# Score products of the second attention layer issued for two jobs at a time in every second slot of TensorE

## The chip, the cores and the metric

The kernel runs on one core of one Trainium2 chip. The metric is device time in microseconds (us), and a lower one is better. The profile is one execution taken by the hardware profiler; its engines are TensorE (PE, its weight loads PEld), VectorE (DVE), ScalarE (ACT), GpSimd (POOL) and the DMA queues that SyncE (SP) issues.

## The reference, cut to what matters

Two layers are computed on a tensor of 4 x 512 tokens with 256 features: an attention that learns as it reads, a feed-forward net, a causal attention with 16 heads, and a routed expert net. The change lies in the third of these, whose core is

```python
scores = jnp.einsum('bqhd,bkhd->bhqk', q, k) * scale        # 128 "nope" + 64 "rope" features
scores = jnp.where(causal[None, None], scores, jnp.finfo(scores.dtype).min)
probs = jax.nn.softmax(scores, axis=-1)
out = jnp.einsum('bhqk,bkhd->bqhd', probs, v).reshape(b, s, NH * D_V)
return out @ Wo
```

The 128 nope features of a key come from a latent of 64 numbers, so the kernel multiplies the key weights into the query first. A score is then a product over 64 latent features plus a product over 64 rope features.

## The kernel before

**Tiling.** `stage_rest` works on 16 batches n (`batches`), each one sample b and one tile of 128 query rows q, in the order q = 1, 3, 0, 2 of each sample. Because of the causal mask a batch needs 128 x (q + 1) keys, so the widths are 256, 512, 128 and 384 for n mod 4 = 0, 1, 2, 3. A batch has eight jobs of two heads, p = 0 to 7; job t = 8n + p, 128 in all (`SLOTS`). Each engine walks through the slots t = 0 to 127 in an order written out by hand.

**A job on the engines.** `score(t)` issues four products on TensorE: latent and rope part for heads e = 0 and e = 1, whose operands lie in rows 0 to 63 and 64 to 127 (lines 2098 and 2101). They go to one of two pairs of PSUM banks (`t % AHEAD`). On VectorE, `largest(t)` (L2454) moves the two score tiles to SBUF and finds their row maxima (`maxed`), `turn(t - 2)` (L2468) transposes the finished probabilities of job t - 2, and `invert(t)` (L2473) takes reciprocals of the sums. On ScalarE, `exponential(t)` (L2354) makes the exponentials. On GpSimd, `normalize(t)` (L2707) scales them. `score(t)` reuses the banks of job t - 2 and waits for `maxed` of job t - 2, head by head.

**Fills.** The rest of TensorE's work is put between the scores by `Plan`, by slot p of the batch: at p = 0, 1 the rope queries of batch n + 1 (L2056, `project_q`); at 2, 3 the weighing of the values of batch n - 1 (`weigh`, L2118, products of 32 rows; one part at p = 2 where n mod 4 = 3); at 4, 5 (3, 4 where n mod 4 = 3) the latent queries of batch n + 1 (L2056); at 6, 7 the output product of batch n - 1 (`project_out`, L2132), at 6, 7 of n mod 4 = 0 also the next sample's values (L2064), at 6 of n mod 4 = 2 its keys (L2073, 64 rows), and at 7 of n = 0, 2, 6, 10, 14 transposes of a norm (L1591). Batch 0 has no weighing and no output; batch 15 makes no queries, and has its output product at 3, 4. Fills use four other banks in turn.

**What the other engines do with a fill.** In its slot, ScalarE first does `exponential(t)`, then takes what was filled in slot t - 1 (`take_rope` L2342, `take_latent` L2346, the value rows L1979, the keys L2334, a norm L1604), and takes the weighed sum (`take_out`, L2363, semaphore `oT_taken`) in the slot after the last part of `weigh`. It is strictly in order, so `exponential(t + 1)` stands behind these takes. On VectorE, the gating of an output (`gate_out`, L2494) stands at the end of slot p = 0, before `largest` of p = 1; the rotation of the keys (L2483, L2484) in slot p = 1 of n mod 4 = 3; the rotation of rope queries (L2479) in p = 4, 5; sums and normalization of a norm (L1566, L1584) in p = 1 and p = 4 of n = 0, 2, 6, 10, 14. The first latent fill and `project_out` need `oT_taken`.

Of the kernel before, what the change touches and what calls it, by code (L numbers as in the profile page):

```python
# [1826 lines left out]
def stage_rest(k):  # L1827
# [8 lines left out]
    AHEAD = 2  # L1836
# [4 lines left out]
    SLOTS = NP * NB  # L1841
# [99 lines left out]
    def wait_taken(eng, *what):  # L1941
        eng.wait_ge(taken[banks.bank(*what)], banks.count(*what))
# [12 lines left out]
    def width(n):  # L1955
        return P * (batches[n][1] + 1)
# [28 lines left out]
    with nc.Block() as block:  # L1985
        @block.tensor
        def _(pe):
# [63 lines left out]
            def project_q(what, w, n, half):  # L2051
                b, cols = tokens(n)
                out = claim(what, n, half)
                for i in range(HP):
                    for kt in range(KT):
                        mm = nc.tensor.matmul(out[:, P * i:P * i + P], w[:, kt, HP * half + i, :], k.hT[:, kt, b, cols],  # L2056
                                              start=(kt == 0), stop=(kt == KT - 1))
                mm.then_inc(made_of(what, n, half), 1)

            def project_value(b, half):  # L2060
                out = claim("value", b, half)
                pe.wait_ge(norms.taken, norms.done(LN1A + b, 1))
                for kt in range(KT):
                    mm = nc.tensor.matmul(out[:], w_val[kt][:, P * half:P * half + P], k.hT[:, kt, b, :],  # L2064
                                          start=(kt == 0), stop=(kt == KT - 1))
                mm.then_inc(made_of("value", b, half), 1)
# [9 lines left out]
            def turn_norm(g):  # L2076
                for kt in range(KT):
                    out = claim("norm", g, kt)
                    norms.turn(pe, g, kt, out)

            def score(t):
                n, p = divmod(t, NP)
                b = batches[n][0]
                if t == 0:
                    pe.wait_ge(first_rows, 2)
                if t == 1:
                    pe.wait_ge(gated_made, 2 * len(ITEMS))
                if p % HP == 0:
                    wait_taken(pe, "latent", n, p // HP)
                    pe.wait_ge(s["q_roped"], 2 * n + p // HP + 1)  # L2090
                    if n % QT == 0:
                        pe.wait_ge(s["ckv_taken"], 2 * (b + 1))
                        pe.wait_ge(keys_spread[p // HP], MOVE * (b + 1))
                halves = [slice(LORA * e, LORA * e + LORA) for e in range(2)]
                for e, rows in enumerate(halves):
                    if t >= AHEAD:
                        pe.wait_ge(s["maxed"], 2 * (t - AHEAD) + e + 1)
                    nc.tensor.matmul(score_bank[t % AHEAD][e][:, 0:width(n)], q_latent[rows, n % 2, p, :],  # L2098
                                     ckvT[rows, b % 2, 0:width(n)], start=True, stop=False)
                for e, rows in enumerate(halves):  # L2100
                    nc.tensor.matmul(score_bank[t % AHEAD][e][:, 0:width(n)], q_rope[rows, n % 2, p, :],  # L2101
                                     keys[b % 2][rows, p // 2, 0:width(n)], start=False, stop=True).then_inc(s["scored"], 1)

            def weigh(n, part, parts):
                b, blocks = batches[n][0], blocks_of(n)
                lo, hi = blocks * part // parts, blocks * (part + 1) // parts
                if part == 0:
                    pe.wait_ge(s["turned"], NP * (n + 1))
                    if b > 0:
                        wait_taken(pe, "value", b, 1)  # L2110
                    for last in banks.before_sum(n):
                        clear(last)
                src = turned_of[batches[n][1]]
                for j in range(lo, hi):
                    for e in range(2):
                        for i in range(ROWS):
                            rows = slice(BLK * i, BLK * i + BLK)
                            mm = nc.tensor.matmul(av[LORA * e:LORA * e + LORA, i, :], val[rows, b % 2, j, :], src[rows, j, e, :, :],  # L2118
                                                  start=(j == 0), stop=(j == blocks - 1))
                if part == parts - 1:  # L2120
                    mm.then_inc(s["weighed"], 1)

            def project_out(n, part):
                out = filled("out", n)
                if part == 0:
                    if n < NB - 1:
                        clear(banks.previous("out", n))
                    pe.wait_ge(s["oT_taken"], n + 1)
                elif n == NB - 1:
                    pe.wait_ge(s["oT_taken"], NB + 1)  # L2130
                for p in range(HP * part, HP * part + HP):
                    mm = nc.tensor.matmul(out[:, 0:D], oT[:, p, :], w_vo[:, p, :], start=(p == 0), stop=(p == NP - 1))  # L2132
                if part == 1:
                    mm.then_inc(made_of("out", n), 1)
# [112 lines left out]
            for n, (b, q) in enumerate(batches):  # L2247
                m, more = n % QT, n + 1 < NB
                for p in range(NP):
                    t = NP * n + p  # L2250
                    if t + AHEAD < SLOTS:
                        score(t + AHEAD)
                    part = p - plan.weigh[m]
                    if n > 0 and 0 <= part < plan.parts[m]:
                        weigh(n - 1, part, plan.parts[m])
                    for half in range(2):
                        if n > 0 and p == plan.out_at(n)[half]:
                            project_out(n - 1, half)
                    for half in range(2):
                        if more and p == plan.rope[m][half]:  # L2260
                            project_q("rope", w_rope, n + 1, half)
                        if more and p == plan.latent[m][half]:
                            project_q("latent", w_abs, n + 1, half)
                    for half in range(2):
                        if b + 1 < B and m in plan.value and p == plan.value[m][half]:
                            project_value(b + 1, half)
                    if b + 1 < B and m in plan.key and p == plan.key[m]:
                        project_keys(b + 1)
                    if n in plan.norms and p == plan.norm:
                        turn_norm(plan.norms[n])  # L2270
# [662 lines left out]
```

## Time and profile before

| | before |
|---|---|
| median of 3 runs | 1076.84 us (1074.63 to 1078.26) |
| profiled execution, its own time | 1076.94 us |
| its span | 1075.1 us |
| PE busy in the span | 1016.1 us (95%) |
| DVE busy | 703.8 us (65%) |
| ACT busy | 546.1 us (51%) |
| POOL busy | 433.7 us (40%) |
| the change's stretch, first score to last | 575.5 to 1018.4 us |

A row of a timeline reads: start, duration, engine, line, operation, output <- inputs, shapes, count, and in brackets how long the engine had been idle before it and what released it. Successive matmuls overlap in their listed durations, so the time that one costs TensorE is the distance to the start of the next.

### The profile page before, as it was taken

How to read it: one execution, taken by the hardware profiler on the slowest of the kernel's cores; microseconds unless marked ns; L12 is line 12 of the kernel's file. 1: busy time of each engine (PE TensorE's matmuls, PEld its weight loads, DVE VectorE, ACT ScalarE, POOL GpSimd, SP SyncE). 2: the span in 40 equal slices, each digit the busy share in tenths (PEclk: the TensorE clock that was granted, in tenths of full speed). 3: DMA queues.
4: the chain of work that ended last, by engine and by line, in shares of the span. 5: the costliest groups of instructions: out<-in, count | busy, mean ns of one | idle time of the engine just before them, and what ended most of it. 6: DMA issues, size and time to landing. Idle time of an engine off the chain costs nothing.

```text
span 1075.1 us, 25979 instructions
## 1 busy us (share of the span) xinstructions
PE 1016.1 (95%) x10226; PEld 739.7 (69%) x10226; DVE 703.8 (65%) x2121; ACT 546.1 (51%) x1418; POOL 433.7 (40%) x391
## 2 busy tenths in 40 slices
PE   6788999999999999999999999999999999999978
PEld 4567888888878546655667576766767686758646
DVE  4888898898899713122225675747584767667774
ACT  2667777777778531212132543545454545444441
POOL 1222033134145411010106474747475756778610
PEclk9999999999999999999999899999999999999999
DMA  9150000000000009100013011200120003000202
GB/s 322 44 185 2 1 0 0 0 0 0 1 2 2 1 1 294 46 1 1 1 30 70 15 27 31 64 7 21 36 65 22 21 22 79 22 21 22 80 2 80
DMA packets 27887, 44.03 MB, mean 41 GB/s; under 512 B 6928, under 2 KB 16912, under 8 KB 26896
## 3 DMA queue, kind: packets, MB, share of 16 engines
q1 hardware_dynamic: 27792, 42.71, 13.5%
q8 instruction: 66, 1.08, 0.4%
q14 instruction: 29, 0.24, 0.1%
HBM read 21.98 MB, written 2.10 MB: 22 GB/s over the span
## 4 chain that ended last, share of the span: by engine, by line
PE 53%; DVE 5%; ACT 2%; issue 1%; POOL 0%; DVEq 0%
PE quad L2056 10%; PE quad L1705 8%; PE quad L2098 7%; PE quad L2118 7%; PE quad L2101 6%; PE quad L2000 5%; PE quad L2132 5%; PE quad L2196 1%; PE quad L2064 1%; ACT act_probs L2354 1%; PE quad L1591 1%; DVE act_probs L2454 1%; ACT act_probs L2363 1%; PE quad L2019 1%; DVE x_pairs L2484 1%
## 5 line engine op out<-in xcount | busy, mean ns | idle before, releaser
L2707 POOL TENSOR_TENSOR act_probs<-act_probs,rden 128x512 f32<-128x512 f32 (+3 forms) x128 | 171.0, 1339 | 155.7 <-DVE rden L2473 155.6
L2354 ACT ACTIVATE act_probs<-act_probs,neg_max 128x256 f32<-128x256 f32 (+3 forms) x256 | 140.8, 552 | 82.9 <-DVE neg_max L2454 82.6
L2056 PEld LDWEIGHTS quad<-hT,ug_queries 128*128 128x128 f32 x1024 | 120.5, 194 | 30.6 <-issue 18.6
L2056 PE MATMUL quad<-hT,ug_queries 128*128 128x128 f32 x1024 | 132.2, 283 | 3.0 <-ACT act_probs L2363 2.2
L2454 DVE CUSTOM_DVE_ANT_0 act_probs<-quad,mask 128x256 f32<-128x256 f32 (+3 forms) x256 | 115.1, 486 | 6.8 <-PE quad L2101 6.1
L1705 PE MATMUL quad<-hT,ug_raw_switch 128*128 128x512 f32 x256 | 115.8, 602 | 0.0
L2098 PE MATMUL quad<-ckvT,ug_raw_switch 64*128 64x512 f32 (+3 forms) x512 | 105.8, 480 | 6.9 <-DVE neg_max L2454 6.9
L2473 DVE RECIPROCAL rden<-den 128x2 f32<-128x2 f32 x128 | 20.6, 161 | 120.2 <-ACT act_probs L2354 120.1
L1720 DVE SCALAR_TENSOR_TENSOR act_probs<-quad,ws_up,silu_keys 128x512 f32<-128x512 f32 x32 | 24.0, 750 | 102.4 <-ACT silu_keys L1715 102.4
L1705 PEld LDWEIGHTS quad<-hT,ug_raw_switch 128*128 128x128 f32 x256 | 48.0, 192 | 55.7 <-issue 55.5
L1715 ACT ACTIVATE silu_keys<-quad,ws_gate 128x512 f32<-128x512 f32 x32 | 22.0, 687 | 120.5 <-PE quad L1705 120.5
L2468 DVE STREAM_TRANSPOSE wq_wo<-act_probs 128x1024 f32<-128x1024 f32 (+1 forms) x64 | 70.8, 1106 | 3.1 <-POOL act_probs L2707 3.1
L2098 PEld LDWEIGHTS quad<-ckvT,ug_raw_switch 64*128 64x128 f32 x512 | 41.7, 186 | 39.8 <-issue 20.6
L2132 PE MATMUL quad<-down_keys,act_probs 128*128 128x256 f32 x256 | 63.5, 392 | 0.8 <-ACT act_probs L2363 0.8
L1426 POOL TENSOR_TENSOR hidden<-gate_silu,hb 128x256 f32<-128x256 f32 x16 | 12.0, 753 | 124.5 <-ACT hb L969 124.5
L2132 PEld LDWEIGHTS quad<-down_keys,act_probs 128*128 128x128 f32 x256 | 46.1, 189 | 19.2 <-issue 11.4
L2000 PE MATMUL quad<-down_raw_out,act_probs 128*128 128x256 f32 x256 | 56.1, 379 | 2.0 <-PEq L1510 2.0
L2000 PEld LDWEIGHTS quad<-down_raw_out,act_probs 128*128 128x128 f32 x256 | 48.4, 190 | 10.1 <-issue 3.7
L2118 PE MATMUL quad<-wq_wo,latent_rows 32*64 32x256 f32 x1792 | 53.0, 378 | 2.4 <-DVE ug_raw_switch L2500 1.6
L1206 DVE SCALAR_TENSOR_TENSOR q_bf<-quad,silu_keys 128x512 bf16<-128x512 f32 x72 | 46.2, 683 | 5.3 <-PE quad L645 5.1
L2354 ACT ACTIVATION_READ_ACCUMULATOR act_probs<-act_probs,neg_max 128x1 f32 x256 | 48.3, 189 | 0.0
L2118 PEld LDWEIGHTS quad<-wq_wo,latent_rows 32*64 32x64 f32 x1792 | 41.0, 131 | 10.3 <-issue 3.6
(332 smaller groups left out, 2317.6 us busy)
## 6 DMA issues: line engine op xcount, KB each, us to landing
rope_swapped<-gate SPq DMA_DIRECT2D x120, 64.0 KB, 2.0
ug_raw_switch<-in_wmod SPq DMA_DIRECT2D x4, 512.0 KB, 6.3
x_pairs<-in_x SPq DMA_DIRECT2D x4, 512.0 KB, 7.0
x_rows<-x_pairs SPq DMA_DIRECT2D x8, 256.0 KB, 5.0
wq_wo<-in_wq_nopeT SPq DMA_DIRECT2D x1, 2048.0 KB, 8.6
wq_wo<-in_wo SPq DMA_DIRECT2D x1, 2048.0 KB, 12.8
down_raw_out<-x_pairs SPq DMA_DIRECT2D x16, 128.0 KB, 2.3
ug_queries<-in_switch_w SPq DMA_DIRECT2D x1, 2048.0 KB, 7.6
```

Of the source, the lines that this page charges most:

```text
L1206: nc.vector.scalar_tensor_tensor(q_bf[:, q, :], bank[q][:], ca_b2, a_bf[:, q, :], ALU.mult, ALU.add).then_inc(taken[q], 1)
L1705: mm = k.nc.tensor.matmul(k.bank[2 * (m % 2) + w][:], self.w_ug[:, w, kt, P * m:P * m + P], k.hT[:, kt, 2 * i:2 * i + 2, 4 * C * u:4 * C * ...
L2000: mm = nc.tensor.matmul(bank[4 + q // 2][:, D * (q % 2):D * (q % 2) + D], act_t[:, m, P * q:P * q + P], w_down[:, ffn.place(m), :], start= ...
L2056: mm = nc.tensor.matmul(out[:, P * i:P * i + P], w[:, kt, HP * half + i, :], k.hT[:, kt, b, cols], start=(kt == 0), stop=(kt == KT - 1))
L2098: nc.tensor.matmul(score_bank[t % AHEAD][e][:, 0:width(n)], q_latent[rows, n % 2, p, :], ckvT[rows, b % 2, 0:width(n)], start=True, stop=F ...
L2101: nc.tensor.matmul(score_bank[t % AHEAD][e][:, 0:width(n)], q_rope[rows, n % 2, p, :], keys[b % 2][rows, p // 2, 0:width(n)], start=False, ...
L2118: mm = nc.tensor.matmul(av[LORA * e:LORA * e + LORA, i, :], val[rows, b % 2, j, :], src[rows, j, e, :, :], start=(j == 0), stop=(j == bloc ...
L2132: mm = nc.tensor.matmul(out[:, 0:D], oT[:, p, :], w_vo[:, p, :], start=(p == 0), stop=(p == NP - 1))
L2354: nc.scalar.activation(tile, tile, ACT.Exp, bias=neg_max[:, r, e:e + 1], scale=-1.0, accum_out=den[:, r, e:e + 1])\
L2454: nc.vector.tensor_tensor_reduce(probs[:, t % RING, e, 0:cols], score_bank[t % AHEAD][e][:, 0:cols], mask[:, L - cols:L], -QK_SCALE, 3e38, ...
L2468: nc.vector.transpose(turned_of[batches[n][1]][:, :, :, p, :].rearrange("p j e c -> p e j c"), probs[:, t % RING, :, 0:width(n)].rearrange ...
L2707: nc.gpsimd.tensor_tensor(tile, tile, rden[:, t % RING, :].unsqueeze(2).to_broadcast([P, 2, cols]), ALU.mult)\
```

## The change

At every even slot t, TensorE now issues `score(t + 2)` and `score(t + 3)` one behind the other, and at odd slots none; the fills of slots t and t + 1 then follow each other. The waits inside `score` are as before, so the second of the pair waits for `maxed` of job t + 1, and the number of products is the same. The other engines' programs are the same.

```diff
                 for p in range(NP):
                     t = NP * n + p
-                    if t + AHEAD < SLOTS:
+                    if t % 2 == 0 and t + AHEAD < SLOTS:
                         score(t + AHEAD)
+                        score(t + AHEAD + 1)
                     part = p - plan.weigh[m]
```

TensorE from p = 4 of batch 1 (width 512) to p = 7, before: ckvT products (L2098) and key products (L2101) are the scores, `hT,ug_queries` the latent queries, `down_keys,act_probs` the output product.

```order
L2098 MATMUL quad<-ckvT,ug_raw_switch 128x512 x2
L2101 MATMUL quad<-silu_keys,ug_raw_switch 128x512 x2
L2056 MATMUL quad<-hT,ug_queries 128x128 x8
L2098 MATMUL quad<-ckvT,ug_raw_switch 128x512 x2
L2101 MATMUL quad<-silu_keys,ug_raw_switch 128x512 x2
L2056 MATMUL quad<-hT,ug_queries 128x128 x8
L2098 MATMUL quad<-ckvT,ug_raw_switch 128x128 x2
L2101 MATMUL quad<-silu_keys,ug_raw_switch 128x128 x2
L2132 MATMUL quad<-down_keys,act_probs 128x256 x4
L2098 MATMUL quad<-ckvT,ug_raw_switch 128x128 x2
L2101 MATMUL quad<-silu_keys,ug_raw_switch 128x128 x2
L2132 MATMUL quad<-down_keys,act_probs 128x256 x4
```

The same slots of the changed kernel:

```order
L2098 MATMUL quad<-ckvT,ug_raw_switch 128x512 x2
L2101 MATMUL quad<-silu_keys,ug_raw_switch 128x512 x2
L2098 MATMUL quad<-ckvT,ug_raw_switch 128x512 x2
L2101 MATMUL quad<-silu_keys,ug_raw_switch 128x512 x2
L2056 MATMUL quad<-hT,ug_queries 128x128 x16
L2098 MATMUL quad<-ckvT,ug_raw_switch 128x128 x2
L2101 MATMUL quad<-silu_keys,ug_raw_switch 128x128 x2
L2098 MATMUL quad<-ckvT,ug_raw_switch 128x128 x2
L2101 MATMUL quad<-silu_keys,ug_raw_switch 128x128 x2
L2132 MATMUL quad<-down_keys,act_probs 128x256 x8
```

The first score of batch 2's second job moved ahead of both output products, and the two latent fills stand together behind both scores.

TensorE from p = 2 of batch 3 (width 384) to the scores of batch 4 (width 256), before:

```order
L2098 MATMUL quad<-ckvT,ug_raw_switch 128x384 x2
L2101 MATMUL quad<-silu_keys,ug_raw_switch 128x384 x2
L2118 MATMUL quad<-x_pairs,latent_rows 64x256 x32
L2098 MATMUL quad<-ckvT,ug_raw_switch 128x384 x2
L2101 MATMUL quad<-silu_keys,ug_raw_switch 128x384 x2
L2056 MATMUL quad<-hT,ug_queries 128x128 x8
L2098 MATMUL quad<-ckvT,ug_raw_switch 128x384 x2
L2101 MATMUL quad<-silu_keys,ug_raw_switch 128x384 x2
L2056 MATMUL quad<-hT,ug_queries 128x128 x8
L2098 MATMUL quad<-ckvT,ug_raw_switch 128x384 x2
L2101 MATMUL quad<-silu_keys,ug_raw_switch 128x384 x2
L2098 MATMUL quad<-ckvT,ug_raw_switch 128x256 x2
```

and in the changed kernel:

```order
L2118 MATMUL quad<-x_pairs,latent_rows 64x256 x32
L2056 MATMUL quad<-hT,ug_queries 128x128 x8
L2098 MATMUL quad<-ckvT,ug_raw_switch 128x384 x2
L2101 MATMUL quad<-silu_keys,ug_raw_switch 128x384 x2
L2098 MATMUL quad<-ckvT,ug_raw_switch 128x384 x2
L2101 MATMUL quad<-silu_keys,ug_raw_switch 128x384 x2
L2056 MATMUL quad<-hT,ug_queries 128x128 x8
L2098 MATMUL quad<-ckvT,ug_raw_switch 128x256 x2
L2101 MATMUL quad<-down_raw_out,ug_raw_switch 128x256 x2
```

The first latent fill now stands right behind the weighing, and the second right before the scores of the next batch; before, a score stood between them in both places.

## Rows read from the trace of the kernel before

**Rows 1.** Busy time in a window: window, length, PE, PEld, DVE, ACT, POOL, PEclk, DMA.

```profile
680.00:780.00 100.00, 99.07 (x1099) 69.79 (x1095) 61.67 (x197) 47.66 (x140) 59.94 (x49) 1.00 0.13 30
```

**Rows 2.** Timeline of PE, two rope slots of batch 9 (width 512).

```profile
839.73 1.13 PE L2098 MATMUL quad<-ckvT,ug_raw_switch 64*128 64x512 f32 x4
...
841.65 2.05 PE L2056 MATMUL quad<-hT,ug_queries 128*128 128x128 f32 x16
843.63 1.13 PE L2098 MATMUL quad<-ckvT,ug_raw_switch 64*128 64x512 f32 x4
```

**Rows 3.** Timeline of PE: a score behind a score, and one between fills, width 256.

```profile
576.44 0.60 PE L2098 MATMUL quad<-ckvT,ug_raw_switch 64*128 64x256 f32 x4
...
577.30 0.38 PE L2098 MATMUL quad<-ckvT,ug_raw_switch 64*128 64x256 f32 x1
...
804.66 0.70 PE L2098 MATMUL quad<-ckvT,ug_raw_switch 64*128 64x256 f32 x4
...
805.73 2.05 PE L2056 MATMUL quad<-hT,ug_queries 128*128 128x128 f32 x16
```

**Rows 4.** Timeline of PE: a value fill behind a score, and one behind a fill.

```profile
600.22 1.12 PE L2064 MATMUL quad<-hT,wk_nopeT 128*128 128x512 f32 x2
...
602.14 0.70 PE L2098 MATMUL quad<-ckvT,ug_raw_switch 64*128 64x512 f32 x2
...
828.46 1.02 PE L2064 MATMUL quad<-hT,wk_nopeT 128*128 128x512 f32 x2
...
830.27 0.70 PE L2098 MATMUL quad<-ckvT,ug_raw_switch 64*128 64x512 f32 x2
```

**Rows 5.** Timeline, batch 9 to 10: latent take, exponential, reciprocal, maxima, next score.

```profile
855.29 0.60 ACT L2346 ACTIVATE ug_raw_switch<-quad 128x512 f32<-128x512 f32 x1 [1.40 <-PE quad L2056]
855.79 0.71 ACT L2354 ACTIVATE act_probs<-act_probs,neg_max 128x512 f32<-128x512 f32 x1
...
857.33 0.17 DVE L2473 RECIPROCAL rden<-den 128x2 f32<-128x2 f32 x1 [0.27 <-ACT act_probs L2354]
857.45 0.69 DVE L2454 CUSTOM_DVE_ANT_0 act_probs<-quad,mask 128x512 f32<-128x512 f32 x1
...
858.06 0.69 DVE L2454 CUSTOM_DVE_ANT_0 act_probs<-quad,mask 128x512 f32<-128x512 f32 x1
...
859.09 0.38 PE L2098 MATMUL quad<-ckvT,ug_raw_switch 64*128 64x128 f32 x2
```

**Rows 6.** Timeline, batch 11 (width 384): exponential and reciprocal behind the second latent take.

```profile
912.55 0.61 ACT L2354 ACTIVATE act_probs<-act_probs,neg_max 128x384 f32<-128x384 f32 x1
...
913.88 0.17 DVE L2473 RECIPROCAL rden<-den 128x2 f32<-128x2 f32 x1 [0.76 <-ACT act_probs L2354]
```

**Rows 7.** Timeline, slot p = 0 of batch 10 (width 128): gating, then maxima.

```profile
864.33 0.42 DVE L2494 TENSOR_TENSOR attn_gated<-quad,gate 128x256 f32<-128x256 f32 x1 [1.27 <-PE quad L2132]
...
864.80 0.29 DVE L2454 CUSTOM_DVE_ANT_0 act_probs<-quad,mask 128x128 f32<-128x128 f32 x1
```

**Rows 8.** Timeline, slot p = 4 of batch 6: the weighed sum is taken, the latent fill waits.

```profile
763.76 0.49 PE L2098 MATMUL quad<-ckvT,ug_raw_switch 64*128 64x128 f32 x4
763.94 1.02 ACT L2363 ACTIVATE act_probs<-quad 128x1024 f32<-128x1024 f32 x1 [6.18 <-PE quad L2118]
...
765.01 0.38 PE L2056 MATMUL quad<-hT,ug_queries 128*128 128x128 f32 x1 [0.54 <-ACT act_probs L2363]
```

**Rows 9.** Timeline, slot p = 2 of batch 11: maxima behind the key rotation, the waiting score.

```profile
900.51 0.54 DVE L2454 CUSTOM_DVE_ANT_0 act_probs<-quad,mask 128x384 f32<-128x384 f32 x1
...
901.21 0.97 PE L2098 MATMUL quad<-ckvT,ug_raw_switch 64*128 64x384 f32 x3 [1.16 <-DVE neg_max L2454]
```

**Rows 10.** Timeline and windows: two long idle times of PE, and the clock behind one.

```profile
478.07 1.06 PE L1591 MATMUL quad<-eye,norm_xn 128*128 128x128 f32 x8 [2.53 <-DVE norm_xn L1584]
...
592.11 1.56 PE L2098 MATMUL quad<-ckvT,ug_raw_switch 64*128 64x256 f32 x4 [2.78 <-DVE neg_max L2454]
...
592.00:596.00 4.00, 3.90 (x15) 3.22 (x16) 3.62 (x16) 2.67 (x9) 2.55 (x2) 0.50 0.00 0
```

## The prediction, made before the changed kernel ran

> **What bounds the kernel now.** I read first the windows of busy time, for the engine that is never idle: over 100 us in the middle of the attention TensorE is busy 99.07 us at full clock, VectorE 61.7, ScalarE 47.7, GpSimd 59.9 [rows 1]. So TensorE sets the pace there, and what it does between its products counts. Then TensorE's timeline, reading distances between starts: at width 512 a score takes 841.65 - 839.73 = 1.92 us and a rope fill 843.63 - 841.65 = 1.98 [rows 2]. Last, the timeline of ScalarE and VectorE, to see how late each `maxed` comes, because the change moves the second score of a pair up to where it needs one.
>
> **The gain: switches between kinds of product.** At width 256 a score behind a score takes 577.30 - 576.44 = 0.86, a score between fills 805.73 - 804.66 = 1.07 [rows 3]: going from 128 (or 32) rows to 64 and back costs the score about 0.2. On the other side a value fill behind a score takes 602.14 - 600.22 = 1.92, and behind a fill 830.27 - 828.46 = 1.81 [rows 4], so a fill pays too, about 0.1 at each end. Taking both scores together and both fills together removes two of four switches, about 0.4 us a pair. Where only one slot has a fill nothing is saved; where the fills are of two kinds half of it. By the plan 63 pairs are formed: 53 have fills of one kind in both slots, 4 weighing beside something else (batches 3, 7, 11, 15; 0.2 each). Of the 53, the last pair of batches 2, 6 and 10 has the 64-row key product at the end of its first fill; that touched a score and now touches 128-row products, so it saves nothing. 50 x 0.4 + 4 x 0.2 = 20.8 us is the gain if nothing waits.
>
> A second gain: at p = 4 of width 128 the latent fill waits for `take_out` (763.94 to 765.01 while the score between lasts only 0.65) [rows 8]. It idles 0.6 now; two scores last 1.1 instead of 0.65, which hides 0.45 of it. At p = 2 of these batches I take a further 0.25 for the last rope take, at width 256 0.2. Nothing in the trace shows a pair's exact cover; the bounds are 0 and the full idle.
>
> Here a page speaks against the size. The rows put a switch at 0.2 us [rows 3, 4]. The Trainium skill, TensorE: Matmul & The Clock Gate, Single matmul latency, says that a matmul standing alone pays a fixed (398 / 2.4) = 166 ns that a stream hides. By that estimate each of some 104 switches gives 0.03 less, and the sum below would end 3.5 us higher. I go by the rows.
>
> **The price: the second score needs `maxed` of the job before.** Let P be the start of a pair. After scores and first fill, ScalarE takes that fill and only then makes the exponential; VectorE inverts, and then runs the maxima that the next pair's second score waits for. At width 512: fill end to take 0.1 (as from a product's end to its gating [rows 7]), take to exponential 0.50, to reciprocal 1.54, to maxima 0.12, both maxima 858.06 + 0.69 - 857.45 = 1.30 [rows 5]: 3.57 us. Meanwhile TensorE has the second fill, 1.79 without its switch, and the first score of the next pair. The wait is 3.57 + 0.24 (semaphore and reload, from 901.21 against the maxima of 900.51 to 901.05 [rows 9]) less 1.79 and less that score. A score is 0.2 + 1.72 x width / 512. So:
> - width stays 512: 3.81 - 1.79 - 1.92 = 0.10. Widths 384, 256, 128 come out at 0.04 or nothing by the same chain (reciprocal 1.33 behind the exponential at 384 [rows 6]).
> - **512 to 128** (last pair of batches 1, 5, 9, 13): 3.81 - 1.79 - 0.65 = 1.37.
> - **384 to 256** (last pair of batches 3, 7, 11): the latent fills stand at p = 3, 4, so the second ends exactly at the next P. 0.1 + 0.50 + 1.33 + 0.12 + 1.03 + 0.24 = 3.32, less a score of 1.07: 2.25.
> - **p = 0**: `largest` of p = 1 stands behind `gate_out`, which waits for the output product that ends at P. Gating starts 0.10 after P, maxima 0.47 later, and at width 128 they last 0.50 [rows 7]. 0.45 + 0.50 + 0.24 - 0.65 = 0.54 (0.45 is what most batches show for the two starts together). At 256: 0.39, at 512: 0.08.
> - **Weighing, then a latent or output product, with nothing between** (pair p = 2 of batches 3, 7, 11, 15): `take_out` starts 0.18 after the weighing and lasts 1.02, and the fill follows: 1.25 us, 765.01 - 763.76 [rows 8].
>
> **Sum, by kind of batch**, against the profiled time:
> - Batches 4, 8, 12: 4 x -0.40, second gain -0.2, p = 0 +0.4: -1.4 each, -4.1.
> - Batches 1, 5, 9, 13: 4 x -0.40, three small waits +0.3, +1.37 at the end: about 0, -0.2 together.
> - Batches 2, 6, 10, 14, three pairs: -1.20 - 0.45 - 0.25 + 0.54 + 0.1: -1.27 each, -5.1. Last pair of 14: -0.4.
> - **Last pair of 2, 6, 10 with batches 3, 7, 11.** Now VectorE rotates keys, is late, and TensorE waits 1.16 [rows 9]. The key fill moves behind another 1.29 us score, so key takes, `exponential` and `gate_out` come later, and the norm transposes wait for the gating: +0.45. The two pairs up to that wait therefore win nothing; then the pair's second score waits for maxima whose start follows the first's by 0.6 (to the exponential) + 1.33 + 0.12 [rows 6], while a late first score and its reload cover part: +0.86. Then +1.25, later +2.25. Against these stand -0.2, -0.1 and -0.4. Together +4.2 each, +12.6.
> - Batch 0: one score waits 2.78 us for maxima behind a norm [rows 10]. Before, a latent fill of 1.98 stood in front of that score; now it is the second of its pair, and the fill comes behind it. The idle grows to some 5 us. The wait itself ends about 0.8 later, since ScalarE's rope takes shift VectorE's work; 0.8 + 1.98 - 0.4 (last pair): +2.35, rounded, with the clock as it was (half clock behind the wait [rows 10]).
> - Batch 15 and the tail: the output product waits 1.25, the jobs there are paced by VectorE: +0.9 (0 to 1.3).
>
> -4.1 - 0.2 - 5.1 - 0.4 + 12.6 + 2.35 + 0.9 = +6.05. 1076.94 + 6.05 = 1083.0. The profiled time is 0.1 above the median, so this holds for the median too.
>
> **Rivals.**
> *TensorE stays the only bound.* For it: VectorE and ScalarE have 38% and 52% idle in the window [rows 1]. Against it: the waits come from the order behind the takes, not from lack of time. It gives 1076.9 - 20.8 - 3.4 = 1053.
> *Half of the price.* If the stretch of batches 3, 7, 11 costs +2 instead of +4.2 each, because the 1.16 us wait of now [rows 9] moves instead of growing, the sum is -0.6: 1076, no change.
> *The clock falls in the new waits* (the other side, and further). Two idles of 2.53 and 2.78 us stand before a clock of 0.50 (1.2 of 2.4 GHz); 1.16 at 901 did not lower it [rows 9, 10]. The new wait of 2.25 us lies between. In batch 0 a rope-size fill takes twice its time at half clock. If the clock falls in each of the three places, TensorE loses 2 to 3 us each time: 1083 + 8 = 1091. [...] The Trainium skill, TensorE: Matmul & The Clock Gate, A second HAM failure mode, holds that frequent short idles between groups of products already make the clock swing; no row here shows that.
> *Small waits everywhere.* The 0.0 to 0.1 of steady pairs could be 0.3, for 40 pairs: 1083 + 10 = 1093.
>
> **How the numbers follow.** Forecast as summed, 1079 to 1087: 0.53. TensorE bound, about 1053 to 1068: 0.09. Half of the price, 1070 to 1079: 0.20. Clock: 0.12. Small waits: 0.06. The range leaves out the first and the upper ends: 1071 to 1092. A measurement tells 0.3%, 3.2 us, from no change, so slower means above 1080.1: 0.68, within: 0.21, faster: 0.11.
>
> **What would show it.** Right: two rope fills in a row in about 3.77 us; L2098 waiting for `neg_max` 1.4 us at 512 to 128, 2.2 us at 384 to 256, 0.5 us at p = 1 of width 128; L2056 waiting 1.2 us for L2363 in batches 3, 7, 11; batch 9 about as long as before, batches 4, 8, 12 shorter by 1.4. Wrong: no waits of L2098 over 0.5 us, or a switch that costs less than 0.1, or `exponential` not held behind the takes.

## The result and the profile after

The changed kernel takes 1085.82 us at the median of 6 runs (1083.34 to 1089.06); the kernel before, timed beside it, 1076.42 (1074.63 to 1078.26). The ratio is 1.0091, with a 95% interval of 1.0072 to 1.011: slower by 9.4 us, which is small but clear of noise. The profiled execution took 1088.14 us, 11.2 more than that of before.

The page of the changed kernel, busy time of each engine (time, share of the span, instructions), and two groups of TensorE products with what they waited for (time and mean of one, then idle time ahead of them):

```profile
PE 1012.9 (93%) x10226; PEld 751.4 (69%) x10226; DVE 704.0 (65%) x2121; ACT 545.9 (50%) x1418; POOL 434.7 (40%) x391
...
L2098 PE MATMUL quad<-ckvT,ug_raw_switch 64*128 64x512 f32 (+3 forms) x512 | 111.8, 470 | 18.5 <-DVE neg_max L2455 17.7
L2056 PE MATMUL quad<-hT,ug_queries 128*128 128x128 f32 x1024 | 124.7, 280 | 4.4 <-ACT act_probs L2364 3.6
```

The same two groups on the page of the kernel before:

```profile
L2098 PE MATMUL quad<-ckvT,ug_raw_switch 64*128 64x512 f32 (+3 forms) x512 | 105.8, 480 | 6.9 <-DVE neg_max L2454 6.9
L2056 PE MATMUL quad<-hT,ug_queries 128*128 128x128 f32 x1024 | 132.2, 283 | 3.0 <-ACT act_probs L2363 2.2
```

TensorE is busy 3.2 us less than before and idle 14.4 us more, so the span is 11.2 us longer: something was saved, and more than all of it went into waiting. L2098, the scores, waits 17.7 us for row maxima, where it waited 6.9; L2056 waits 3.6 us for the take of the weighed sum, where it waited 2.2. (Lines are one higher here than in the kernel before, and two to five higher than there in the experiments.)

**The saving.** Timeline of TensorE, batch 9 (width 512): the two rope fills, the scores issued in slot 2, those issued in slot 4, the two latent fills, and the first score issued in slot 6. They answer to [rows 2]:

```profile
846.24 3.84 PE L2056 MATMUL quad<-hT,ug_queries 128*128 128x128 f32 x32
850.01 1.13 PE L2098 MATMUL quad<-ckvT,ug_raw_switch 64*128 64x512 f32 x4
...
857.40 1.13 PE L2098 MATMUL quad<-ckvT,ug_raw_switch 64*128 64x512 f32 x4
...
861.03 3.84 PE L2056 MATMUL quad<-hT,ug_queries 128*128 128x128 f32 x32
864.80 0.49 PE L2098 MATMUL quad<-ckvT,ug_raw_switch 64*128 64x128 f32 x4
```

Two fills now take 850.01 - 846.24 = 3.77 us, against twice 1.98; two scores 861.03 - 857.40 = 3.63, against twice 1.92. The pair of slots 4 and 5, from 857.40 to 864.80, is 7.40 us long, 0.40 less than its 7.80 of before.

**The waits.** First 512 to 128, from batch 9 to 10 (answers to [rows 5]): ScalarE's take, the exponential, VectorE's reciprocal and first maxima, the second score of the pair.

```profile
863.12 0.60 ACT L2347 ACTIVATE ug_raw_switch<-quad 128x512 f32<-128x512 f32 x1 [3.12 <-PE quad L2056]
863.62 0.71 ACT L2355 ACTIVATE act_probs<-act_probs,neg_max 128x512 f32<-128x512 f32 x1
...
865.15 0.17 DVE L2474 RECIPROCAL rden<-den 128x2 f32<-128x2 f32 x1 [1.81 <-ACT act_probs L2355]
865.27 0.69 DVE L2455 CUSTOM_DVE_ANT_0 act_probs<-quad,mask 128x512 f32<-128x512 f32 x1
...
866.03 0.98 PE L2098 MATMUL quad<-ckvT,ug_raw_switch 64*128 64x128 f32 x3 [0.51 <-DVE neg_max L2455]
866.64 0.18 PEld L2098 LDWEIGHTS quad<-ckvT,ug_raw_switch 64*128 64x128 f32 x1 [0.32 <-DVE neg_max L2455]
```

Take to exponential 0.50, exponential to reciprocal 1.53: the chain as forecast. The score waits twice, once for each head's maxima, and the bracket of 0.51 is only the first of the two; the whole delay is read from the distances below.

Second, batch 11 (answers to [rows 6, 8, 9]): the second score waits, then weighing and latent fill with the take of the weighed sum between them; at the end of the block the 384 to 256 case.

```profile
907.18 0.97 PE L2098 MATMUL quad<-ckvT,ug_raw_switch 64*128 64x384 f32 x3 [1.55 <-DVE neg_max L2455]
...
909.14 2.12 PE L2098 MATMUL quad<-ckvT,ug_raw_switch 64*128 64x384 f32 x4
...
912.48 3.60 PE L2118 MATMUL quad<-x_pairs,latent_rows 32*64 32x256 f32 x64
917.28 2.05 PE L2056 MATMUL quad<-hT,ug_queries 128*128 128x128 f32 x16 [1.21 <-ACT act_probs L2364]
```

```profile
924.13 0.60 ACT L2347 ACTIVATE ug_raw_switch<-quad 128x512 f32<-128x512 f32 x1 [2.97 <-PE quad L2056]
...
924.63 0.60 ACT L2355 ACTIVATE act_probs<-act_probs,neg_max 128x384 f32<-128x384 f32 x1
...
926.07 0.56 DVE L2455 CUSTOM_DVE_ANT_0 act_probs<-quad,mask 128x384 f32<-128x384 f32 x1
...
926.69 0.96 PE L2098 MATMUL quad<-ckvT,ug_raw_switch 64*128 64x256 f32 x3 [1.53 <-DVE neg_max L2455]
```

The wait of 1.55 us was 1.16 before [rows 9]. Third, batch 0 (answers to [rows 10]): a wait of 5.18 us, where 2.78 stood.

```profile
593.21 1.56 PE L2098 MATMUL quad<-ckvT,ug_raw_switch 64*128 64x256 f32 x4 [5.18 <-DVE neg_max L2455]
```

**The clock.** Windows of batch 11 (window, length, PE busy, PEld, DVE, ACT, POOL, granted clock, DMA):

```profile
905.50:909.00 3.50, 1.95 (x10) 1.06 (x8) 3.49 (x8) 1.79 (x5) 2.12 (x3) 1.00 0.33 80
909.00:912.40 3.40, 3.37 (x9) 1.96 (x8) 3.39 (x11) 1.31 (x4) 2.58 (x2) 0.50 0.33 77
912.40:915.80 3.40, 3.40 (x65) 1.96 (x64) 0.12 (x1) 0.00 (x0) 0.00 (x0) 0.50 0.83 193
915.80:919.20 3.40, 2.19 (x24) 1.86 (x16) 0.75 (x3) 2.21 (x5) 0.50 (x1) 1.00 0.51 118
```

Behind the 1.55 us wait the granted clock is 0.50, that is 1.2 of 2.4 GHz, for 6.8 us. The weighing takes 3.60 us there and 1.98 in batch 3. Batches 3 and 7 have the same wait of 1.55 and no such stretch.

The table, called the pair table below, takes the start of the first score of every pair of slots (every second score) in both traces; its numbers are the changes of the distances from one such start to the next, in us, added up before rounding. A batch has four pairs: slots 0 and 1, 2 and 3 ("at the weighing"), 4 and 5, 6 and 7 ("the last pair").

| part of the kernel | forecast | after - before |
|---|---|---|
| up to the first score | 0 | +0.29 |
| batch 0 | +2.35 | +0.39 + 1.81 - 0.54: +1.67 |
| batches 1, 5, 9, 13 | -0.2 | +0.51 (last pair +0.99 each) |
| batches 2, 6, 10, 14, three pairs | -5.1 | -1.19 - 0.13 - 1.20 - 0.77: -3.28 |
| last pair of batch 14 | -0.4 | -0.40 |
| last pair of 2, 6, 10 with batches 3, 7, 11 | +12.6 | +4.14 + 4.14 + 7.15: +15.43 |
| batches 4, 8, 12 | -4.1 | -4.08 |
| batch 15 and the tail | +0.9 | +1.06 |
| sum | +6.05 | +11.2 |

### The profile page after: what moved, and what is told of

The parts are those of the page before. It is cut to its first block, busy times and chain, and to the rows that moved or that the text cites. A ratio compares the mean times of both kernels' runs of the same rounds, so it can differ in the third digit from the quotient of the medians.

```text
span 1086.3 us, 25979 instructions
## 1 busy us (share of the span) xinstructions
PE 1012.9 (93%) x10226; PEld 751.4 (69%) x10226; DVE 704.0 (65%) x2121; ACT 545.9 (50%) x1418; POOL 434.7 (40%) x391
## 4 chain that ended last, share of the span: by engine, by line
PE 51%; DVE 6%; ACT 4%; issue 2%; DMA 0%; POOL 0%; SPq 0%; DVEq 0%
PE quad L2056 9%; PE quad L1705 7%; PE quad L2098 7%; PE quad L2118 7%; PE quad L2101 5%; PE quad L2000 5%; PE quad L2132 4%; ACT act_probs L2355 2%; PE quad L2196 1%; DVE act_probs L2455 1%; PE quad L2064 1%; PE quad L1591 1%; DVE x_pairs L2485 1%; ACT act_probs L2364 1%; PE quad L2019 1%
## 5 line engine op out<-in xcount | busy, mean ns | idle before, releaser
L2056 PEld LDWEIGHTS quad<-hT,ug_queries 128*128 128x128 f32 x1024 | 118.2, 194 | 20.4 <-issue 12.3
L2098 PE MATMUL quad<-ckvT,ug_raw_switch 64*128 64x512 f32 (+3 forms) x512 | 111.8, 470 | 18.5 <-DVE neg_max L2455 17.7
L2056 PE MATMUL quad<-hT,ug_queries 128*128 128x128 f32 x1024 | 124.7, 280 | 4.4 <-ACT act_probs L2364 3.6
L2098 PEld LDWEIGHTS quad<-ckvT,ug_raw_switch 64*128 64x128 f32 x512 | 50.8, 187 | 54.3 <-DVE neg_max L2455 28.1
L2132 PE MATMUL quad<-down_keys,act_probs 128*128 128x256 f32 x256 | 60.9, 387 | 2.0 <-ACT act_probs L2364 2.0
L2101 PE MATMUL quad<-silu_keys,ug_raw_switch 64*128 64x256 f32 (+3 forms) x256 | 52.3, 440 | 0.0
L2101 PE MATMUL quad<-down_raw_out,ug_raw_switch 64*128 64x256 f32 (+3 forms) x256 | 50.2, 431 | 0.0
```

## The experiments

The theory: each pair saves some 0.4 us of TensorE where both scores come without a wait, and the loss sits in a few places, behind ScalarE's strict order (take ahead of exponential) and VectorE's (maxima behind the exponential's reciprocal). The rivals: small waits spread over all batches, or a clock that falls because of the new waits. Where a time of "before" is set beside a run, it was timed in the same series: 1077.87, 1076.35 and 1076.40 us in the three series.

### Pairs only where nothing waits, and only where something does

Against the changed kernel (the condition is one line in the kernel):

```diff
-                    if t % 2 == 0 and t + AHEAD < SLOTS:
+                    first = t - t % 2
+                    two = not (m == 3 or (m == 1 and first % NP == 6)
+                        or (m == 2 and first % NP in (0, 6) and n < NB - 2) or (n == 0 and first % NP < 6))
+                    if t + AHEAD < SLOTS and not (two and t % 2):
                         score(t + AHEAD)
-                        score(t + AHEAD + 1)
+                        if two:
+                            score(t + AHEAD + 1)
```

only_costly has the same condition without its `not`.

> Scores go two by two only in the pairs of slots in which I place no new wait; in batches n = 3, 7, 11, 15, in the last pair of batches 1, 5, 9, 13, in the first and last pair of 2, 6, 10 and in the first pairs of batch 0 they go one by one as in the kernel before. My theory (a switch between kinds of product costs 0.2 us, and the losses sit in a few named waits): the pairs' changes as the trace of the changed kernel shows them are -1.36 for each of batches 4, 8, 12, about -1.0 for each of 1, 5, 9, 13, -1.5 for each of 2, 6, 10, 14, and about -0.8 more: -15 us in all, about 1061.5 us. Rival (VectorE runs late everywhere once scores come in pairs, and the loss is spread): the gain is given back in waits of other pairs, 1070 to 1080.

> The complement of the run before: scores go two by two only where I place the waits. My theory: +1.0 for each of batches 1, 5, 9, 13, +0.6 for each of 2, 6, 10, +3.7 for each of 3, 7, 11, +2.2 in batch 0, +2 at the end: +21 us, about 1097, and up to 3 us more for each fall of TensorE's clock. The changes of the two runs then add up to that of the changed kernel (+9). Rival (loss spread over all pairs): about half of the changed kernel's loss, 1080 to 1085.

only_free: 1063.33 us (1062.27 to 1064.95), ratio 0.9873 (0.9848 to 0.9899). only_costly: 1095.09 us (1092.27 to 1097.4), ratio 1.0163 (1.0134 to 1.0192). The pairs that were left single here come from the forecast's list of waits, picked with the trace of the changed kernel at hand. They carry the whole loss; small waits everywhere are refuted, since all other pairs together gain 14.5 us. In the trace of only_free batches 3, 7 and 11 are as long as before to 0.01 us, batches 4, 8, 12 are 4.07 shorter. The kernel was timed again in a later series, as only_free_again:

> The kernel of only_free, beside the others of this call. Everything computed is the reference's. Theory: its time was set by the pairs and not by where the clock happened to fall: 1062 to 1065 again. Rival (a favourable run of the clock): 1066 to 1068, as late_and_free.

1064.37 us (1061.73 to 1066.73), ratio 0.9881 (0.986 to 0.9902).

The two halves don't add up to the whole: -14.5 + 17.2 = +2.7 at the medians, where the whole change costs 9.4. The pair table shows why. The last pair of batches 1, 5, 9, 13 is +0.99 in the changed kernel and -0.40 in only_costly, though its two scores are joined there too. Timeline of only_costly, batch 9 to 10:

```profile
872.64 0.49 PE L2098 MATMUL quad<-ckvT,ug_raw_switch 64*128 64x128 f32 x4
...
873.19 0.39 PE L2098 MATMUL quad<-ckvT,ug_raw_switch 64*128 64x128 f32 x4
```

No wait, and 0.55 us from one score to the next. What differs is the pair before it: there the two latent fills stand apart, so the take of the first and the exponential run ahead of the second. The wait of 512 to 128 belongs to two joined pairs in a row, and either one left single removes it. That is 4 x 1.39 = 5.6 us of the 6.7 that are missing. The forecast's sum for this place holds for the full change only. So the expectation that the two changes add up was wrong.

The clock works the other way and doesn't fill the rest. only_costly has 6.8 us of half clock behind the same 1.53 us wait that leaves the clock up in batch 7 of the full kernel (this pair is +5.26 instead of +1.98), and a shorter stretch at the end of batch 11 (+3.62 instead of +1.98): 4.9 us, where the profiled execution of the full kernel lost 3.0. What else makes up the 6.7 is left open; the medians alone are uncertain by 1 or 2 us (last section). Timeline and windows (with PE alone) of only_costly, the end of batch 7:

```profile
809.75 1.27 PE L2098 MATMUL quad<-ckvT,ug_raw_switch 64*128 64x256 f32 x3 [1.53 <-DVE neg_max L2458]
```

```profile
810.00:813.40 3.40, 3.40 (x11) 0.52 0.01 2
813.40:817.00 3.60, 3.60 (x10) 0.50 0.00 0
```

### The second latent of batches 3, 7, 11 taken behind the exponential

```diff
                 for _, n, half in due(t, 1, "latent"):
-                    take_latent(n, half)
+                    if n % QT > 0 or half == 0:
+                        take_latent(n, half)
+                for _, n, half in due(t, 2, "latent"):
+                    if n % QT == 0 and half == 1:
+                        take_latent(n, half)
```

> The changed kernel, but ScalarE takes the second latent fill of batches 3, 7 and 11 after the next exponential and not before it. My theory: the wait of about 2.2 us of the second score of width 256 was for maxima that stood behind that take; it goes, 3 x -1.98 us: about 1080 against 1085.8. The clock's falls come earlier in these batches and stay. Rival (VectorE or GpSimd has too little time there, whatever ScalarE's order): less than 1 us of it goes, 1084 to 1086.

1080.56 us (1078.51 to 1082.34), ratio 1.0033 (1.002 to 1.0046). The 384 to 256 pair went from +1.98 to +0.18 or +0.19 in all three blocks. Timeline of late_second_latent, batch 11: the exponential now stands ahead of the take, the maxima follow it, and the second score comes 0.97 behind the first with no wait in brackets.

```profile
917.47 0.60 ACT L2355 ACTIVATE act_probs<-act_probs,neg_max 128x384 f32<-128x384 f32 x1
...
918.07 0.70 PE L2098 MATMUL quad<-ckvT,ug_raw_switch 64*128 64x256 f32 x4
918.18 0.60 ACT L2347 ACTIVATE ug_raw_switch<-quad 128x512 f32<-128x512 f32 x1
...
918.32 0.56 DVE L2459 CUSTOM_DVE_ANT_0 act_probs<-quad,mask 128x384 f32<-128x384 f32 x1
...
919.04 0.86 PE L2098 MATMUL quad<-ckvT,ug_raw_switch 64*128 64x256 f32 x3
```

So three takes of ScalarE, moved by one place, are worth 3 x 1.8 = 5.4 us; the median fell by 5.3. That the take ahead of the exponential makes this wait is shown. The half-clock stretch of batch 11 is gone here, and one stands at the weighing of batch 7 instead (that pair is +3.17), behind the same 1.55 us wait.

### All takes of even slots one slot later

```diff
-                for _, n, half in due(t, 1, "rope"):
-                    take_rope(n, half)
+                for later in ((2, 1) if t % 2 == 0 else ()):
+                    for _, n, half in due(t, later, "rope"):
+                        take_rope(n, half)
...
```

(the same for latent, value and key fills)

> The changed kernel, but ScalarE takes every rope, latent, value and key fill of an even slot one slot later, behind the next exponential; TensorE's order is unchanged. My theory: the waits behind the takes go: 3 x -1.98 at 384 to 256, 4 x -0.99 at 512 to 128, 3 x -0.45 where the key takes stand ahead of the exponential, 8 x -0.1 small ones: -12 us, about 1074. What stays: the wait for the weighed sum at p = 3 of batches 3, 7, 11, 15, the gating at p = 0, the key rotation and batch 0. Rival (spread loss or lack of time on VectorE): 1082 to 1086.

1074.3 us (1070.04 to 1075.05), ratio 0.997 (0.9954 to 0.9986), with every pair kept: the theory's 1074. The last pairs of batches 1, 5, 9 and 13 go from +0.99 to -0.40, those of 3, 7 and 11 from +1.98 to +0.19. What stays is +1.81 at the weighing (+3.12 in batch 3, with half clock), where the second score waits 1.55 us for maxima and the latent fill 1.18 for the take of the weighed sum, which this edit doesn't move; and +1.60 in batch 0.

### No pair at the weighing of batches 3, 7, 11, 15

```diff
+                    first = t - t % 2
+                    two = not (m == 3 and first % NP == 2)
```

(and the two scores issued by `two`, as above)

> As the kernel after, but in slots 2 and 3 of batches 3, 7, 11 and 15 the scores are issued one by one as in the kernel before. Everything computed is the reference's. Theory (the weigh pair of these batches costs 1.8 us each, 1.9 in batch 15, and the stretches at half clock follow its longer wait): 4 x 1.8 us, about 7.3 us less than the kernel after, and about 3 us less where the clock also stays up in batch 11: 1076 to 1079. Rival (the clock falls wherever the new waits come, also those behind the second latent): 1079 to 1082, with a half-clock stretch elsewhere in batches 3, 7 or 11.

1082.67 us (1082.36 to 1083.73), ratio 1.0067 (1.0049 to 1.0086): outside what the theory gave. The pairs at the weighing are as long as before again (0.00, from +1.82), which is 4 x 1.8 us back, and the half clock of batch 11 with it; but the pair at the end of the block went from +1.98 to +3.62, +3.67 and +3.67, and what follows the last score pair of batch 15 grew by 2.0, with 6.8 us at half clock from 1046.96. Timeline and window of no_pair_at_weigh3, the end of batch 3, then the same place of the changed kernel:

```profile
687.11 0.96 PE L2098 MATMUL quad<-ckvT,ug_raw_switch 64*128 64x256 f32 x3 [1.53 <-DVE neg_max L2458]
...
688.67 5.34 PE L2132 MATMUL quad<-down_keys,act_probs 128*128 128x256 f32 x16
```

```profile
688.60:692.00 3.40, 3.40 (x9) 2.69 (x9) 1.71 (x6) 1.09 (x4) 2.86 (x3) 0.50 0.00 0
```

```profile
690.34 0.96 PE L2098 MATMUL quad<-ckvT,ug_raw_switch 64*128 64x256 f32 x3 [1.53 <-DVE neg_max L2455]
...
691.88 3.72 PE L2132 MATMUL quad<-down_keys,act_probs 128*128 128x256 f32 x16
```

```profile
692.00:696.00 4.00, 4.00 (x20) 3.28 (x22) 1.95 (x8) 1.09 (x4) 2.95 (x3) 1.00 0.00 0
```

The same 1.53 us wait stands before the same products; in one kernel 16 output products behind it take 5.34 us, at clock 0.50, in the other 3.72, at full clock. The rival of this run was right in kind, and in size but for 0.7 us: where one wait was taken away, half-clock stretches stand behind another.

### Pairs and late takes together

> ScalarE takes the rope, latent, value and key fills of even slots one slot later (behind the next exponential), and the scores are issued in pairs in every pair of slots but three: the weigh pair of batches 3, 7, 11 and 15 (slots 2 and 3), the first pair of batches 2, 6, 10 and 14, and the first three pairs of batch 0. Everything computed is the reference's. Theory (a pair saves about 0.4 us of TensorE wherever neither score has to wait for a row maximum or for ScalarE, and the losses sit only in those three places and behind ScalarE's takings): by the table of pair durations of late_takes, the latent pairs of batches 3, 7, 11 stay at +0.2 each, the remaining pairs keep -0.4 to -1.3; the sum is about -16 to -17 us against the kernel before: about 1060 to 1061. Rival (late takes and pairs interfere: what is taken late holds PSUM and delays a later fill): no better than the pairs without late takes, about 1063 to 1067.

The takes as in late_takes; the pairs by this condition:

```diff
+                    two = not ((m == 3 and first % NP == 2) or (m == 2 and first % NP == 0) or (n == 0 and first % NP < 6))
```

1067.28 us (1066.26 to 1070.54), ratio 0.993 (0.9913 to 0.9947). Faster than before, but 6 to 7 us over the theory and no better than the pairs without late takes, as the rival had it. That what is taken late delays a later fill by holding its bank was not tested. Batches 1, 5, 9, 13 gave the -6.2 us that they should. Batches 3, 7 and 11 cost +2.55 instead of +0.6, of which batch 3 alone +1.65. Part of it is seen: the weighing itself now waits for a take; the rest of batch 3 I can't explain. Timeline of late_and_free, batch 3:

```profile
669.34 0.97 PE L2098 MATMUL quad<-ckvT,ug_raw_switch 64*128 64x384 f32 x3 [1.55 <-DVE neg_max L2459]
...
671.60 1.99 PE L2118 MATMUL quad<-x_pairs,latent_rows 32*64 32x256 f32 x64 [0.32 <-ACT gate L2346]
```

Batch 14 lost 0.8 against only_free. In its profiled execution another 2.3 us came before the first score, with a stretch at half clock at 405.7 us, where the two kernels are the same; only_free_again has such a stretch at 405.5 us, only_free has none.

### The latent fills of batches 3, 7, 11 one slot later

On top of late_and_free, with the scores at the weighing of batches 3, 7 and 11 in pairs again:

```diff
-    latent = ((4, 5), (4, 5), (4, 5), (3, 4))
+    latent = ((4, 5), (4, 5), (4, 5), (4, 5))
```

> As late_and_free, but the two latent groups of a block stand in slots 4 and 5 of batches 3, 7, 11 instead of 3 and 4, and the scores are paired there too (all but the weigh pair of batch 15). Everything computed is the reference's. Theory (the +1.8 us of the weigh pair is the wait of the latent group in slot 3 for ScalarE to take the weighed output, which no score covers when both stand ahead of the weighing): with two scores between weighing and latent the wait goes, and batches 3, 7, 11 gain another 0.4 to 0.5 us each against late_and_free: about 1059 to 1060. Rival (the +1.8 us is the second score's wait for the row maxima beside the weighing): the waits stay, 3 x 1.8 us more than late_and_free: about 1065.

1077.21 us (1074.3 to 1081.32), ratio 1.0015 (1.0002 to 1.0029): the theory fell, and the time is 17 us above what it gave and 12 above its rival. Against the kernel before, the pair at the weighing got 1.4 shorter, the next one 6.16, 4.57 and 6.20 longer. One latent fill of about 2 us only changed its place; the rest is a new wait. Timeline of latents_4_5, batch 3:

```profile
674.48 0.92 PE L2098 MATMUL quad<-ckvT,ug_raw_switch 64*128 64x384 f32 x4
...
674.66 1.02 ACT L2367 ACTIVATE act_probs<-quad 128x1024 f32<-128x1024 f32 x1 [2.66 <-PE quad L2118]
...
675.58 0.60 ACT L2358 ACTIVATE act_probs<-act_probs,neg_max 128x384 f32<-128x384 f32 x1
...
677.57 0.55 DVE L2459 CUSTOM_DVE_ANT_0 act_probs<-quad,mask 128x384 f32<-128x384 f32 x1
...
678.19 1.06 PE L2098 MATMUL quad<-ckvT,ug_raw_switch 64*128 64x384 f32 x3 [2.15 <-DVE neg_max L2459]
```

The wait for the weighed sum is gone, as meant. But its take of 1.02 us stands ahead of the exponential all the same, the cosine multiplication of 0.67 ahead of the maxima, and no fill stands between the weighing and the second score, so TensorE waits 2.15 there. The fill in slot 3 had been the cover for that chain. Two of the three blocks ran at half clock behind this wait, which is the 1.6 us between 6.2 and 4.57.

### Batch 0 with single scores

```diff
+                    two = not (n == 0 and first % NP < 6)
```

> As the kernel after, but the first three pairs of slots of batch 0 issue their scores one by one as before. Everything computed is the reference's. Theory (the first pair costs 0.39 and the third 1.81 us, a wait of 5.18 us for row maxima that stood at 2.78 before): 2.2 us less than the kernel after, 1083 to 1084. Rival (the whole +1.8 belongs to a stretch at half clock that falls into batch 0 either way): no difference, 1085.5 to 1086.5.

1084.79 us (1083.72 to 1088.13), ratio 1.0079 (1.0054 to 1.0104). The first and third pair went from +0.39 and +1.81 to 0.00 and 0.00, and the wait from 5.18 to 2.78 again:

```profile
593.37 1.56 PE L2098 MATMUL quad<-ckvT,ug_raw_switch 64*128 64x256 f32 x4 [2.78 <-DVE neg_max L2458]
```

The places show the 2.2 us, the medians only 1.0: in this execution a stretch at half clock lies in batch 7 (+3.13 instead of +1.81) and not in batch 11, and another of 6.8 us from 1050.23. So the place is shown, and the median by itself would not tell the theory from its rival.

### Late takes only in batches 1, 5, 9, 13

Against the order of takes in late_takes:

```diff
-                for later in ((2, 1) if t % 2 == 0 else ()):
+                for later in [k for k in (2, 1) if (k == 2) == ((t - k) % 2 == 0 and t >= k and (t - k) // NP % QT == 1)]:
```

With the pairs of only_free and the last pair of these four batches.

> As only_free, but ScalarE takes what was filled in the even slots of batches 1, 5, 9 and 13 one slot later, and the last pair of these batches is issued in twos as well. Everything computed is the reference's. Theory (late takes pay in these four batches and cost in batches 2, 3 and 14; in the pair table the four batches sum to -6.2 us with late takes and -3.5 us in only_free): 2.8 us less than only_free: about 1060.5. Rival (a late take in these batches pushes its delay into the batch behind): no better than only_free, 1063 to 1064.

1060.87 us (1059.15 to 1063.09), ratio 0.986 (0.9838 to 0.9881), the lowest median of the study, 15.5 us under before and 3.5 under only_free_again beside it (the ranges of the two overlap). The last pair of the four batches gains 0.40 each, and batches 3, 7, 11 are at 0.00. Against only_free the profiled execution gained 2.0 in the four batches and not 2.8: at their first pair the takes still come from the batch before, in time as ever, and their small waits stay (+0.20 in batch 1, where late_and_free had -0.40). Another 2.7 came from the clock in batch 0 (below), which the kernel doesn't owe to the edit as far as the runs show. So the theory's 1060.5 was met in part by luck.

## Why the prediction was right

The forecast was 1083.0 us in a range of 1071 to 1092, slower with a chance of 0.68; measured were 1085.82, a loss of 0.9%. By its own steps:

- **The gain per pair** was right. 0.40 us in 7.80 [rows 2 to 4], and the pairs of width 512 in slots 4 and 5 show -0.39 or -0.40; in batches 4, 8, 12 the four pairs are 0.00, -0.38, -0.58 and -0.40, together -1.36 for -1.4. The rows, and not the fixed latency of a single product, were the better ground. The Trainium skill, TensorEngine Tiling (Array Packing), Key Properties, says that changing the tiling mode drains TensorE; this trace fits it in that a change has a price, with two 64-row scores in 3.63 us where they took 3.84 apart. That a drain is what the price pays for, no run shows.
- **512 to 128**: 1.37 - 0.40 = +0.97 forecast, +0.99 measured in each of the four batches. Their first pairs are -0.33, but +0.20 in batch 1, which is why the four batches give +0.51 together.
- **The block of batches 3, 7, 11**: +4.2 forecast, +4.14 measured twice, with the parts in their places: +0.43 for the key fill, 0.00, then +1.82 for 0.86 + 1.25 - 0.2, -0.10, and +1.98 for the 384 to 256 case. The third is +7.15; 3.0 of it is the clock.
- **The clock** was the term left out of the sum. The forecast kept it as a rival with three places, and set the new waits between an idle of 1.16 us that left the clock up and idles of 2.53 and 2.78 us that didn't [rows 9, 10]. One of three places fell, behind a wait of 1.55 us. So the rival happened in part: 3.0 of the 5.2 us by which the profiled execution, at +11.2, is over +6.05. For the 2.8 us between forecast and median it can't be said, since only one of the six runs left a trace. The runs also show that the length of the idle was the wrong thing to ask for: see below.
- **The sum itself** has slips that nearly cancel. The chain at width 512 adds up to 3.56, not 3.57. The parts given for batches 1, 5, 9, 13 come to +0.07 each, +0.3 together and not -0.2; those for the block come to +4.1, 12.3 and not 12.6; batches 4, 8, 12 to -4.2. Added as written they give some +6.3 for +6.05. The misses that are left, -0.7 in batch 0 against +1.8 in batches 2, 6, 10, 14 and +0.7 in 1, 5, 9, 13, offset each other in part too, and that is luck.
- **Batches 2, 6, 10, 14, three pairs**: -5.1 forecast, -3.3 measured. Two pieces are short. In batch 6 the weighing, 256 small products in a row, has pauses without a wait for anyone. In batch 14 the second score of slots 2 and 3 waits 0.31 us for its maxima, which VectorE makes late, behind norm sums that hold it from 988.73 to 991.38. Batches 2 and 10 gave -1.19 and -1.20 for -1.27. Timeline of the changed kernel, batch 6:

```profile
760.23 7.47 PE L2118 MATMUL quad<-wq_wo,latent_rows 32*64 32x256 f32 x249
767.99 0.66 PE L2118 MATMUL quad<-wq_wo,latent_rows 32*64 32x256 f32 x7 [0.29 <-issue]
768.58 0.49 PE L2098 MATMUL quad<-ckvT,ug_raw_switch 64*128 64x128 f32 x4
```

  From 760.23 to 768.58 are 8.35 us, where the half before the score of 763.76 [rows 8] took 3.64, from 760.12, and two make 7.28. The same pair was +0.60 here, +0.42 and +0.48 in late_and_free and latents_4_5, and -0.54 and -0.65 in only_free and no_pair_at_weigh3 with the same order of products in it; only_free_again, the very kernel of only_free, has +0.07. So it isn't a price of the order. The profile names `issue`, which is time in which the engine waits for nothing that the profile shows; what it waits for is left open.
- **Batch 0**: +2.35 forecast, +1.67 measured. The place and the cause were right (single_in_batch_0); the 0.8 us by which the wait was to end later is 0.2: 0.39 + 1.81 - 1.98.
- **TensorE as the only bound** was the clean miss among the rivals: it left out that waits for row maxima would go from 6.9 to 17.7 us. *Half of the price* fell too: the block cost its full 4.14. *Small waits everywhere* fell with only_free.

## What to carry to other kernels

When two steps of the busiest engine are joined, the step that comes second arrives earlier by a whole fill, and its input doesn't. Write down, for each place where neighbours differ in size or kind, the chain from the last fill through every in-order engine to that input, and join only where the cover exceeds it: the same edit won 14.5 us where it was applied by such a list (checked against the trace of the full change), and cost 9.4 applied everywhere. Joined steps also act on the next join, so a place is judged with its neighbours as they will be. A take that sits ahead of the next job's exponential on ScalarE is what made the chain long at seven places here. Moving it behind the exponential helped there; in batch 3 of late_and_free the weighing then waited for a take moved so.

## What the runs showed of the hardware that was not expected

**The same wait, with the clock up and down.** Before, a wait of 2.78 us in batch 0 was followed by a clock of 0.50 [rows 10]. In late_in_second the same products wait the same 2.78 us, in the same order, and the clock stays up, which makes this pair 2.68 us shorter. Timeline and windows of late_in_second:

```profile
591.92 0.82 PE L2098 MATMUL quad<-ckvT,ug_raw_switch 64*128 64x256 f32 x3 [2.78 <-DVE neg_max L2459]
```

```profile
588.00:592.00 4.00, 1.22 (x12) 1.03 (x10) 4.00 (x7) 0.10 (x1) 2.98 (x3) 1.00 0.06 14
592.00:596.00 4.00, 4.00 (x28) 3.23 (x30) 3.62 (x14) 3.15 (x11) 2.65 (x3) 1.00 0.00 0
```

The 1.53 us waits at the ends of batches 3 and 7 are other cases of one wait and two clocks. So is the 1.55 us wait at the weighing: a half-clock stretch stands behind it in batch 11 of the changed kernel, in batch 7 of late_second_latent and of single_in_batch_0, in batch 3 of late_takes, and in the other two batches each time not. So the idle time alone doesn't decide, and an edit elsewhere in the kernel came with 1.3 to 3.3 us won or lost at such a wait. What does decide is left open. The Trainium skill, TensorE: Matmul & The Clock Gate, A second HAM failure mode: psum-queue depth-cycling, says that frequent short idles between groups of products make the clock swing; here stretches at half clock came behind single waits of 1.5 us, in some batches and some kernels, and not in others.

**Its size in a comparison.** The runs of one kernel span 1.4 to 7 us. For the changed kernel the mean clock goes with them at the ends: 0.994 in the run of 1083.34 us, 0.991 in that of 1089.06. By estimate a median over 4 to 6 runs carries 1 or 2 us of this: only_free gave 1063.33 and, again, 1064.37. The steady pairs at full clock repeat to 0.01 or 0.02 us from kernel to kernel (-0.38 to -0.40), and such pairs, not the medians, told the terms of the sum apart.
